# Eight transposes of a score tile in one go on TensorE, in a four-layer attention and expert kernel

## The chip, the cores and the metric

The kernel is one program on one core of a Trainium2 chip. The metric is the device time of one execution in microseconds (us), lower is better; the times shown are the median of several runs and their lowest and highest. The profile is one execution taken by the hardware profiler. In it PE is TensorE's matmuls, PEld its weight loads, DVE is VectorE, ACT is ScalarE, POOL is GpSimd, and SP is the engine that issues the DMAs.

## What is computed

The input `x` is 4 x 1024 x 128. Four layers follow, each `x = x + layer(layernorm(x))`: a first attention with relative positions (8 heads of 128), a mixture of 8 experts, a second attention (16 heads of 8, causal), and the same mixture of experts again. Only the first attention is touched:

```python
Q = (q @ w_qs).reshape(B, L, H, Dk).transpose(0, 2, 1, 3) * scale
K = (q @ w_ks).reshape(B, L, H, Dk).transpose(0, 2, 1, 3)
V = (q @ w_vs).reshape(B, L, H, Dv).transpose(0, 2, 1, 3)
attn = jnp.einsum('bnqd,bnkd->bnqk', Q + rel_embed_bias, K)
rel_k = (positions @ w_rel_pos_k).reshape(-1, H, Dk).transpose(1, 0, 2)
attn_pos = relative_shift(jnp.einsum('bnqd,nkd->bnqk', Q + rel_pos_bias, rel_k))
a = jax.nn.softmax(attn + attn_pos, axis=-1)
out = jnp.einsum('bnqk,bnkd->bnqd', a, V)
out = out.transpose(0, 2, 1, 3).reshape(B, L, H * Dv) @ w_out + b_out
```

With B = 4, L = 1024 and H = 8 that is 32 pairs of a head and a batch, each with a 1024 x 1024 score matrix.

## The kernel before, in words

**Tiles and steps.** A score tile is 128 queries by 1024 keys; there are 256 of them, `t` or `s` = 0 to 255, 32 for each head. The first attention runs as one long software pipeline with one step per tile (the loop over `s` in `plan_a`, L84). Four tiles make a quad (512 queries), `qd`; `kq = s % 4` is the place of a step in its quad. In step `s` the kernel computes the scores of tile `s`, the position products of tile `s + 3`, and a quarter of the product of the finished quad before it (`pq = s // 4 - 1`) with V.

**The order.** `plan_a` writes one list of units. PE, ACT, DVE and SP each walk through this same list and issue, for each unit, their own part of it, so that the list is the order of all of them; each waits on semaphores for what the others have to deliver. Nothing is reordered later: where an engine waits in one unit, its parts of all units behind it wait too. The units of a step, in order:

- `s`: six 512-wide matmuls give the scores in PSUM banks 2 and 3 (L612). DVE adds the position scores that a DMA brought into `a_sp`, and takes the minimum of the negated sum (L1201).
- `t` for `ja = 2 kq`: four 128 x 128 transposes (L622) turn one block of 128 keys of the quad's four tiles, into PSUM bank 4; ACT copies it to `a_Ph` in the rounded format (L904). Unit `tlow` is DVE's part: it takes the difference of the bank and `a_Ph` as the low half `a_Pl` (L1207). It stands behind `exp`.
- `pv` (block 7 of the quad before) where `kq` is 0, with ACT's copy of the finished sum to `a_osb` (L910).
- `r` 0: three 384-wide matmuls of the position products for tile `s + 3`; ACT copies them out (L889). `exp`: ACT's exponential of tile `s` (L897). `tlow` for `ja`. `r` 1: three more, copied out by DVE (L1193). `pv` for block `ja - 1`: three 512-wide matmuls with `a_Ph`, `a_Pl` and V (L635 to L637).
- one side unit in bank 7: the next quad's `q` (kq = 0), the transposes and the sum of the quad's output `out` (kq = 1, L643, L1222), a half of the next `k` (kq = 2) or of a `v` (kq = 3). `q`, `k` and `v` are matmuls, a rounded copy by ACT (`q`: two, L874; `k`: L879; `v`: L883) and the low half by DVE (`q`: two, L1174; `k`: L1180; `v`: L1186).
- `t` for `jb = 2 kq + 1`, into bank 5, with ACT's copy; `r` 2 and the DMA that writes the position products to DRAM; the DMA that reads them back skewed for tile `s + 2`; `tlow` for `jb`; `pv` for block `ja`.
- in some steps one or two `rel` units (the position blocks of the next head, also in bank 7), and in others the layer norms and gates of other layers.

**The waits at a transpose group.** Group `n = 8 pq + j` of PE waits until `p_lo` has reached `n - 1`, that is, until DVE has finished `tlow` of group `n - 2`, the last user of the same bank. ACT's copy of it waits until `pv` of block `n - 3` is through, since there are three buffers for `a_Ph`. The `r` 0 of the step with `kq` = 1 is the first that needs the quad's new `q`, and waits for both of its low halves.

```python
                if 8 * qd + j >= 2:
                    e.wait_ge(S["p_lo"], 8 * qd + j - 1)
                for k in range(4):
                    i = e.transpose(ps[:, 4 + j % 2, 128 * k:128 * k + 128],
                                    self.sp[:, (4 * qd + k) % NSP, 128 * j:128 * j + 128], ident[:, :])
```

Names in the rows: `a_sp` scores, `a_Ph` and `a_Pl` the two halves of the turned exponentials, `a_Qh`, `a_Kh`, `a_Vh` and `a_Ql`, `a_Kl`, `a_Vl` the halves of q, k, v, `a_rh` and `a_rl` of the position blocks, `a_rt` position products on their way to DRAM, `a_osb` the output sum, `a_fh` and `a_gh` what the position blocks are made of.

Of the kernel before, what the change touches and what calls it, by code (L numbers as in the profile page):

```python
# [51 lines left out]
def splits(p):  # L52

    return lambda b, bank: [("ln_stats", p, b), ("ln_total", p, b), ("ln_scale", p, b, 0), ("ln_turn", p, b, 0, bank),
                            ("ln_scale", p, b, 1), ("ln_turn", p, b, 1, bank)]


def gates(g, b):
    return [(u, g, b) for u in ("gt_logits", "gt_best", "gt_place", "gt_share", "gt_combine")]


def plan_a():

    p = splits(0)(0, 6) + [("x_bias", 0), ("feat",), ("wv", 0, 0, 7), ("q", 0, 2), ("k", 0, 0, 3), ("wv", 0, 1, 7),
                           ("k", 0, 1, 4)]
    p += [("rel", 0, u, 2 + (3 + i) % 5) for i, u in enumerate((7, 6, 5, 4))]
    p += [("v", 0, half, 2 + (2 + half) % 5) for half in range(2)]
    p += [("rel", 0, u, 2 + (4 + i) % 5) for i, u in enumerate((3, 2, 1, 0))]
    for t in range(3):
        p += [("r", t, 0), ("r", t, 1), ("r", t, 2), ("rout", t)]  # L70
        if t:
            p.append(("rin", t - 1))
    rel_at = {}
    for h in range(1, H):
        for ds, us in {-1: (7,), 1: (6,), 3: (5,), 4: (4, 3), 6: (2,), 8: (1,), 10: (0,)}.items():
            rel_at.setdefault(8 * (4 * h - 1) + ds, []).extend(("rel", h, u, 7) for u in us)
    extra = {}
    for b in range(1, B):
        for i, it in enumerate(splits(0)(b, 7) + [("x_bias", b)]):
            extra.setdefault(i // 4 if b == 1 else 8 * b - 14 + i, []).append(it)  # L80
    for b in range(B - 1):
        for i, it in enumerate(splits(1)(b, 7) + gates(0, b)):
            extra.setdefault(4 * (8 * (H - 1) + 2 * b + 3) + 1 + 3 * i // 4, []).append(it)
    for s in range(NTI + 6):  # L84
        kq, qd, bh, pq = s % 4, s // 4, s // 8, s // 4 - 1
        live, ahead, tlive = s < NTI, s + 3 < NTI, 0 <= pq < NQ
        ja, jb = 2 * kq, 2 * kq + 1
        h1 = s // 32 + 1
        if live and s % 32 == 2 and h1 < H:
            p.append(("load", h1))  # L90
        if live and s % 32 == 8 and h1 < H:
            p.append(("weights", h1))
        if live and s % 32 in (10, 12) and h1 < H:
            p.append(("wv", h1, s % 32 // 2 - 5, 7))
        if live:
            p.append(("s", s))
        if tlive:
            p.append(("t", pq, ja))
        if kq == 0 and 0 < pq <= NQ:
            p.append(("pv", pq - 1, 7))  # L100
        if ahead:
            p.append(("r", s + 3, 0))
        if live:
            p.append(("exp", s))
        if tlive:
            p.append(("tlow", pq, ja))
        if ahead:
            p.append(("r", s + 3, 1))
        if kq and tlive:
            p.append(("pv", pq, ja - 1))  # L110
        if kq == 0 and qd + 1 < NQ:
            p.append(("q", qd + 1, 7))
        if kq == 1 and 0 < pq <= NQ:
            p.append(("out", pq - 1, 7))
        if kq == 2 and live and bh + 1 < NTI // 8:
            p.append(("k", bh + 1, qd % 2, 7))
        if kq == 3 and live:
            if qd % 2 and bh + 1 < NTI // 8:
                p.append(("v", bh + 1, 0, 7))
            if qd % 2 == 0 and bh:  # L120
                p.append(("v", bh, 1, 7))
        if tlive:
            p.append(("t", pq, jb))
        if ahead:
            p += [("r", s + 3, 2), ("rout", s + 3)]
        if s + 2 < NTI:
            p.append(("rin", s + 2))
        if tlive:
            p += [("tlow", pq, jb), ("pv", pq, ja)]
        p += rel_at.get(s, []) + extra.get(s, [])  # L130
    return p
# [116 lines left out]
class Program:  # L248
    def __init__(self, nc, dram):
        self.nc, self.dr = nc, dram  # L250
        self.ctx = ExitStack()
        with self.ctx as ctx:
            self.S = {n: ctx.enter_context(nc.semaphore(n)) for n in SIGNALS}
            self.d_x = [ctx.enter_context(nc.semaphore(f"d_x{b}")) for b in range(B)]
            self.d_rout = [ctx.enter_context(nc.semaphore(f"d_rout{i}")) for i in range(4)]
            self.d_rin = [ctx.enter_context(nc.semaphore(f"d_rin{i}")) for i in range(NSP)]
            self.d_w1 = [ctx.enter_context(nc.semaphore(f"d_w1_{k}")) for k in range(E)]
            self.memory()
            self.plans = plan_a(), plan_f(0), plan_b(), plan_f(1)
            block = ctx.enter_context(nc.Block())  # L260
            block.sync(self.sync)
            block.tensor(self.tensor)
            block.scalar(self.scalar)
            block.vector(self.vector)
            block.gpsimd(self.gpsimd)
# [1233 lines left out]
```

## Time and profile before

| | us |
|---|---|
| device time, median of 3 runs | 3046.62 |
| lowest and highest | 3041.37, 3055.7 |
| the profiled execution's own device time | 3042.59 |
| its span in the trace | 3040.9 |
| PE busy | 2748.4 (90% of the span) |
| DVE busy | 2055.9 (68%) |
| ACT busy | 1735.5 (57%) |
| first attention | from the start to about 1700 |

Busy time of an engine is the union of its instructions, and a PE that is busy need not be at its peak. The timeline gives for each instruction its start, its length and its engine; matmuls overlap, so the pace of PE is read from one start to the next. "[1.42 <-DVE a_Ql L1174]" behind an instruction means that its engine stood idle for 1.42 us before it and which instruction ended that.

### The profile page before, as it was taken

What the parts mean: (1) busy time and instruction counts of PE and PEld (TensorE: products, weight loads), DVE (VectorE), ACT (ScalarE), POOL (GpSimd) and SP (SyncE); (2) the same over time, 40 slices, a digit from 0 to 9 for tenths busy, and PEclk for the clock granted to TensorE, in tenths of its full rate; (3) what the DMA queues carried; (4) which work ended last, traced back from release to release, by engine and by line L of the source; (5) the groups of instructions that cost most, each with busy time, mean ns of one, the idle gap of its engine ahead of it and who ended that gap; (6) DMA issues with size and microseconds to landing.
All of it is one profiled execution on the core that took longest, in us unless ns stands there. A gap on an engine that the chain in (4) does not pass through costs nothing. (4 is left out here: it accounts for less than half of the span.)

```text
span 3040.9 us, 46580 instructions
## 1 busy us (share of the span) xinstructions
PE 2748.4 (90%) x15120; PEld 2169.6 (71%) x15120; DVE 2055.9 (68%) x5219; ACT 1735.5 (57%) x3566; POOL 355.5 (12%) x782
## 2 busy tenths in 40 slices
PE   5999999999999999999999418998898999988999
PEld 4788888888888888888888316775555555554777
DVE  4766666666666666666666428887877777773887
ACT  3665666656666666666555214553666666655454
POOL 0000000000000000000000013341222122222344
PEclk8999999999999999999999759996999998999999
DMA  3554545545555455455443110000000000000000
GB/s 113 179 177 167 189 173 184 181 170 189 184 174 183 171 184 190 167 189 180 172 168 139 53 42 1 1 1 1 1 1 1 1 1 1 1 1 1 8 8 15
DMA packets 92673, 301.04 MB, mean 99 GB/s; under 512 B 10162, under 2 KB 24626, under 8 KB 92338
## 3 DMA queue, kind: packets, MB, share of 16 engines
q1 hardware_dynamic: 92434, 298.06, 28.5%
q8 instruction: 125, 2.05, 0.3%
q14 instruction: 114, 0.93, 0.1%
HBM read 144.93 MB, written 153.09 MB: 98 GB/s over the span
## 5 line engine op out<-in xcount | busy, mean ns | idle before, releaser
L904 ACT ACTIVATE a_Ph<-ps 128x512 fp32r<-128x512 f32 x512 | 305.9, 597 | 419.4 <-PE ps L622 415.0
L982 ACT ACTIVATE r_P<-ps 128x512 f32<-128x512 f32 (+3 forms) x768 | 328.0, 491 | 187.0 <-PE ps L752 182.7
L1201 DVE CUSTOM_DVE_ANT_0 a_sp<-ps,a_sp 128x1024 f32<-128x1024 f32 x256 | 313.1, 1223 | 176.9 <-PE ps L240 171.3
L1207 DVE TENSOR_TENSOR a_Pl<-ps,a_Ph 128x512 fp32r<-128x512 f32 x512 | 350.1, 684 | 11.4 <-ACT a_Ph L904 11.4
L933 ACT ACTIVATE r_y<-ps 128x256 f32<-128x256 f32 x512 | 194.3, 385 | 216.0 <-PE ps L666 213.7
L897 ACT ACTIVATE a_sp<-a_sp,a_nm 128x1024 f32<-128x1024 f32 x256 | 293.2, 1145 | 34.2 <-DVE a_nm L1201 34.1
L622 PE MATMUL ps<-ident,a_sp 128*128 128x128 f32 x2048 | 310.7, 274 | 0.0
L664 PE MATMUL ps<-r_Wh,p_xh 128*128 128x512 f32 x512 | 220.9, 431 | 93.9 <-DVE r_Wl L1236 46.6
L238 PE MATMUL ps<-a_rh,a_Qh 128*128 128x384 f32 x768 | 299.5, 390 | 4.7 <-DVE a_Ql L1174 4.2
L732 PE MATMUL ps<-r_K,r_Q 128*128 128x512 f32 (+3 forms) x768 | 282.7, 403 | 18.2 <-DVE r_mx L1363 12.8
L622 PEld LDWEIGHTS ps<-ident,a_sp 128*128 128x128 f32 x2048 | 250.2, 141 | 52.1 <-issue 1.0
L752 PE MATMUL ps<-r_Q,r_K 128*128 128x512 f32 (+3 forms) x768 | 254.2, 376 | 30.3 <-ACT r_P L982 28.4
L1363 DVE CUSTOM_DVE_ANT_0 ps<-ps,maskq 128x256 f32<-128x256 f32 (+3 forms) x512 | 244.8, 506 | 52.9 <-PE ps L732 51.8
L240 PE MATMUL ps<-a_rh,a_Ql 128*128 128x384 f32 x768 | 262.0, 341 | 0.0
L889 ACT ACTIVATE a_rt<-ps 128x384 f32<-128x384 f32 x512 | 252.9, 494 | 14.3 <-PE ps L240 13.7
L239 PE MATMUL ps<-a_rl,a_Qh 128*128 128x384 f32 x768 | 259.4, 338 | 0.0
L732 PEld LDWEIGHTS ps<-r_K,r_Q 128*128 128x128 f32 x768 | 145.1, 198 | 157.2 <-DVE r_mx L1363 80.0
L452 POOL TENSOR_TENSOR r_acc<-r_acc,r_yk 128x256 f32<-128x256 f32 x256 | 189.0, 738 | 329.2 <-DVE r_yk L1268 318.1
L464 POOL TENSOR_SCALAR_AFFINE_SELECT r_P<-r_P 128x128 f32<-128x128 f32 x512 | 153.1, 309 | 555.6 <-ACT r_P L982 547.3
L635 PE MATMUL ps<-a_Ph,a_Vh 128*128 128x512 f32 x512 | 210.0, 410 | 7.5 <-DVE a_Pl L1207 7.0
L440 POOL TENSOR_TENSOR wst<-wst,wr 128x512 f32<-128x512 f32 x4 | 5.0, 1262 | 1792.0 <-DMA wr<-in_w1r 1792.0
L1367 DVE TENSOR_REDUCE r_mx<-ps 128x1 f32<-128x512 f32 x256 | 176.1, 688 | 49.9 <-PE ps L732 48.5
(219 smaller groups left out, 6215.7 us busy)
## 6 DMA issues: line engine op xcount, KB each, us to landing
scr<-a_rt SPq DMA_DIRECT2D x256, 576.0 KB, 3.1
a_sp<-scr SPq DMA_DIRECT2D x256, 512.0 KB, 4.3
x<-in_q SPq DMA_DIRECT2D x4, 512.0 KB, 9.0
wst<-in_w1t SPq DMA_DIRECT2D x8, 256.0 KB
out<-x SPq DMA_DIRECT2D x4, 512.0 KB, 3.2
wr<-in_w1r SPq DMA_DIRECT2D x8, 254.0 KB
a_gst<-in_w_rel SPq DMA_DIRECT2D x8, 96.0 KB, 3.0
a_sp<-in_feat SPq DMA_DIRECT2D x1, 768.0 KB, 7.6
```

The lines of the kernel that those rows point to most:

```text
L238: e.matmul(out, lh, rh, start=True, stop=False)
L239: e.matmul(out, lh, rl, start=False, stop=False)
L240: return e.matmul(out, ll, rh, start=False, stop=True)
L622: i = e.transpose(ps[:, 4 + j % 2, 128 * k:128 * k + 128], self.sp[:, (4 * qd + k) % NSP, 128 * j:128 * j + 128], ident[:, :])
L732: e.matmul(ps[:, bank, 0:w], self.Q[:, b % 2, g, 128 * I:128 * I + 128], self.K[:, b % 2, q, 512 * part:512 * part + w], start=True, stop= ...
L752: e.matmul(ps[:, bank, off:512], self.K[:, b % 2, q, 128 * J:128 * J + 128], self.Q[:, b % 2, g, 512 * ch + off:512 * ch + 512], start=Tru ...
L889: e.activation(self.rt[:, t % 2, 384 * k:384 * k + 384], ps[:, (3 * t + k) % 2, 0:384], ACT.Copy).then_inc(S["r_act"], 1)
L897: e.activation(w, w, ACT.Exp, bias=self.nm[:, t % 8:t % 8 + 1], scale=-1.0, accum_out=self.ls[:, t % 16:t % 16 + 1]).then_inc(S["p_exp"], 1)
L904: e.activation(self.Ph[:, n % 3, :], ps[:, 4 + n % 2, :], ACT.Copy).then_inc(S["p_hi"], 1)
L982: e.activation(self.P[:, pt, off:512], ps[:, bank, off:512], ACT.Exp).then_inc(S["b_exp"], 1)
L1201: e.tensor_tensor_reduce(out=w, in0=ps[:, 2:4, :].rearrange("p a n -> p (a n)"), in1=w, scale=-1.0, scalar=3e38, op0=ALU.add, op1=ALU.min, ...
L1207: e.tensor_tensor(self.Pl[:, n % 3, :], ps[:, 4 + n % 2, :], self.Ph[:, n % 3, :].bitcast(F32), ALU.subtract).then_inc(S["p_lo"], 1)
```

## The change

The unit `t` for `jb` moves from behind the side unit to directly behind the `t` for `ja`. All other units keep their places, `tlow` and `pv` for `jb` among them.

```diff
         if tlive:
-            p.append(("t", pq, ja))
+            p += [("t", pq, ja), ("t", pq, jb)]
         if kq == 0 and 0 < pq <= NQ:
             p.append(("pv", pq - 1, 7))
...
                 p.append(("v", bh, 1, 7))
-        if tlive:
-            p.append(("t", pq, jb))
         if ahead:
             p += [("r", s + 3, 2), ("rout", s + 3)]
```

The lines of the changed kernel behind L121 have numbers smaller by 2. The following pieces are from the fourth head.

PE, a step with `kq` = 1, which has the `out` unit (L643), before:

```order
L622 MATMUL ps<-ident,a_sp 128x128 x4
L238 MATMUL ps<-a_rh,a_Qh 128x384
L239 MATMUL ps<-a_rl,a_Qh 128x384
L240 MATMUL ps<-a_rh,a_Ql 128x384
L238 MATMUL ps<-a_rh,a_Qh 128x384
L239 MATMUL ps<-a_rl,a_Qh 128x384
L240 MATMUL ps<-a_rh,a_Ql 128x384
L635 MATMUL ps<-a_Ph,a_Vh 128x512
L636 MATMUL ps<-a_Pl,a_Vh 128x512
L637 MATMUL ps<-a_Ph,a_Vl 128x512
L643 MATMUL ps<-ident,a_osb 128x128 x4
L622 MATMUL ps<-ident,a_sp 128x128 x4
```

and with the change:

```order
L620 MATMUL ps<-ident,a_sp 128x128 x8
L236 MATMUL ps<-a_rh,a_Qh 128x384
L237 MATMUL ps<-a_rl,a_Qh 128x384
L238 MATMUL ps<-a_rh,a_Ql 128x384
L236 MATMUL ps<-a_rh,a_Qh 128x384
L237 MATMUL ps<-a_rl,a_Qh 128x384
L238 MATMUL ps<-a_rh,a_Ql 128x384
L633 MATMUL ps<-a_Ph,a_Vh 128x512
L634 MATMUL ps<-a_Pl,a_Vh 128x512
L635 MATMUL ps<-a_Ph,a_Vl 128x512
L641 MATMUL ps<-ident,a_osb 128x128 x4
L236 MATMUL ps<-a_rh,a_Qh 128x384
```

The second group of transposes now stands ahead of nine matmuls and the output's transposes, instead of behind them.

ACT, a step with `kq` = 0, which has the copy of the output sum (L910) and the two copies of `q` (L874), before:

```order
L904 ACTIVATE a_Ph<-ps 128x512
L910 ACTIVATE a_osb<-ps 128x512
L889 ACTIVATE a_rt<-ps 128x384
L897 ACTIVATE a_sp,a_ls<-a_sp,a_nm 128x1024
L874 ACTIVATE a_Qh<-ps,a_bias 128x512 x2
L904 ACTIVATE a_Ph<-ps 128x512
L889 ACTIVATE a_rt<-ps 128x384
```

and with the change:

```order
L902 ACTIVATE a_Ph<-ps 128x512 x2
L908 ACTIVATE a_osb<-ps 128x512
L887 ACTIVATE a_rt<-ps 128x384
L895 ACTIVATE a_sp,a_ls<-a_sp,a_nm 128x1024
L872 ACTIVATE a_Qh<-ps,a_bias 128x512 x2
L887 ACTIVATE a_rt<-ps 128x384
```

The second copy to `a_Ph` now stands ahead of the exponential and of the two copies of `q`.

DVE keeps its order. From the same step with `kq` = 0 to the start of the next:

```order
L1193 COPY a_rt<-ps 128x384
L1174 SCALAR_TENSOR_TENSOR a_Ql<-ps,a_bias,a_Qh 128x512 x2
L1207 TENSOR_TENSOR a_Pl<-ps,a_Ph 128x512
L1201 ISA a_sp,a_nm<-ps,a_sp 128x1024
L1201 ISA a_nm 128x1
```

Nothing moved here: the second `a_Pl` of the step stands behind the two low halves of `q`.

## Rows read from the trace of the kernel before

**Rows 1.** Windows: busy us of PE, PEld, DVE, ACT, POOL, then clock, DMA

```profile
450.00:750.00 300.00, 294.77 (x1695) 260.02 (x1694) 195.27 (x375) 190.46 (x367) 0.00 (x0) 1.00 0.51 178
...
1350.00:1650.00 300.00, 286.84 (x1614) 250.86 (x1613) 196.06 (x438) 182.89 (x347) 0.00 (x0) 0.98 0.49 170
```

**Rows 2.** Waits of PE, 150 to 1700 us: total, times, longest

```profile
PE ps L238 <- DVE a_Ql L1174: 20.6, 15, 1.4
```

**Rows 3.** Timeline, PE, two steps: start, length, engine, line

```profile
995.14 0.40 PE L637 MATMUL ps<-a_Ph,a_Vl 128*128 128x512 f32 x1
...
1000.18 0.60 PE L622 MATMUL ps<-ident,a_sp 128*128 128x128 f32 x4
...
1000.54 0.42 PE L238 MATMUL ps<-a_rh,a_Qh 128*128 128x384 f32 x1
...
1000.80 0.34 PE L239 MATMUL ps<-a_rl,a_Qh 128*128 128x384 f32 x1
...
1000.97 0.34 PE L240 MATMUL ps<-a_rh,a_Ql 128*128 128x384 f32 x1
```

**Rows 4.** Timeline, ACT, the first of these steps

```profile
994.87 0.60 ACT L904 ACTIVATE a_Ph<-ps 128x512 fp32r<-128x512 f32 x1 [2.01 <-PE ps L622]
...
995.57 0.60 ACT L910 ACTIVATE a_osb<-ps 128x512 f32<-128x512 f32 x1
...
996.11 0.49 ACT L889 ACTIVATE a_rt<-ps 128x384 f32<-128x384 f32 x1
...
996.49 1.14 ACT L897 ACTIVATE a_sp<-a_sp,a_nm 128x1024 f32<-128x1024 f32 x1
...
997.62 1.26 ACT L874 ACTIVATE a_Qh<-ps,a_bias 128x512 fp32r<-128x512 f32 x2
```

**Rows 5.** Timeline, DVE, end of the first step

```profile
998.91 1.41 DVE L1174 SCALAR_TENSOR_TENSOR a_Ql<-ps,a_bias,a_Qh 128x512 fp32r<-128x512 f32 x2 [1.73 <-ACT a_Qh L874]
...
1000.24 0.68 DVE L1207 TENSOR_TENSOR a_Pl<-ps,a_Ph 128x512 fp32r<-128x512 f32 x1
```

**Rows 6.** Timeline, the same place in an early and a late quad

```profile
193.20 0.68 DVE L1207 TENSOR_TENSOR a_Pl<-ps,a_Ph 128x512 fp32r<-128x512 f32 x1
...
193.50 0.42 PE L238 MATMUL ps<-a_rh,a_Qh 128*128 128x384 f32 x1
...
1531.49 0.68 DVE L1207 TENSOR_TENSOR a_Pl<-ps,a_Ph 128x512 fp32r<-128x512 f32 x1
...
1531.79 0.42 PE L238 MATMUL ps<-a_rh,a_Qh 128*128 128x384 f32 x1
```

**Rows 7.** Timeline, bank 7: a position block behind q, one behind k

```profile
645.61 1.41 DVE L1174 SCALAR_TENSOR_TENSOR a_Ql<-ps,a_bias,a_Qh 128x512 fp32r<-128x512 f32 x2 [1.73 <-ACT a_Qh L874]
...
647.08 0.39 PE L238 MATMUL ps<-a_fh,a_gh 96*128 96x256 f32 x1 [1.42 <-DVE a_Ql L1174]
...
861.60 0.69 DVE L1180 TENSOR_TENSOR a_Kl<-ps,a_Kh 128x512 fp32r<-128x512 f32 x1 [1.23 <-ACT a_Kh L879]
...
862.43 0.31 PE L238 MATMUL ps<-a_fh,a_gh 96*128 96x256 f32 x1
```

**Rows 8.** Timeline, DVE and PE, a step with k

```profile
1010.20 0.68 DVE L1207 TENSOR_TENSOR a_Pl<-ps,a_Ph 128x512 fp32r<-128x512 f32 x1
...
1012.16 0.42 PE L238 MATMUL ps<-a_rh,a_Qh 128*128 128x384 f32 x1
```

**Rows 9.** Timeline and windows, output transposes with a score group behind them

```profile
1002.39 0.60 PE L643 MATMUL ps<-ident,a_osb 128*128 128x128 f32 x4
...
1002.82 0.60 PE L622 MATMUL ps<-ident,a_sp 128*128 128x128 f32 x4
...
1003.18 0.42 PE L238 MATMUL ps<-a_rh,a_Qh 128*128 128x384 f32 x1
...
1003.44 0.33 PE L239 MATMUL ps<-a_rl,a_Qh 128*128 128x384 f32 x1
...
1002.39:1003.18 0.79, 0.79 (x10) 0.79 (x8) 0.79 (x3) 0.79 (x2) 0.00 (x0) 1.00 0.82 239
```

## The prediction

> **What bounds the kernel now.** I read first the windows of the first attention, then PE's waits there, then the timeline of two neighbouring steps on PE, ACT and DVE. The windows [rows 1] show PE busy 294.77 of 300 us in the middle of the stage, and 286.84 of 300 near its end, at a granted clock of 1.00 and 0.98, with DVE at about 195 of 300 and ACT at 183 to 190. So PE's stream of matmuls sets the pace and hardly ever pauses. At 5.23 idle us in 300, a stage of some 1,600 us has about 28 us that any new order could bring back. Most of it is in [rows 2]: from 150 to 1700 us PE waits 20.6 us behind the low halves of q, in 15 places. No wait at a transpose group is among the waits. The gain of a change of order is bounded by these 28 us; its cost is whatever pauses it makes. The question is whether the second transpose group, moved forward by half a step, still finds its PSUM bank free and what its copy pushes back on ACT.
>
> **The work itself.** Nothing is added or removed: 2,048 transposes, 512 copies, 512 low halves, and the same matmuls and DMAs. A group of four is 0.36 us from its start to that of the next matmul (1000.18 to 1000.54 [rows 3]).
>
> **Step one, the bank.** Group jb writes bank 5, which is free when DVE has made the low half of the group two before, the jb of the previous step. That low half is the last thing DVE does in a step. Before, PE reached the group half a step later, so that it was always free. Now PE reaches it at the end of the ja group. In a step with kq = 1 the place is 1000.54, where the position products start before [rows 3]. The low half that it needs starts at 1000.24 and takes 0.68 [rows 5], so it ends at 1000.92, and would be 0.38 us late even if nothing else moved. The reason is the q unit of the step before: two copies on ACT, then two low halves on DVE from 998.91 for 1.41 us [rows 5], and only then the low half of jb. In [rows 6] the same distance is 193.88 less 193.50 = 0.38 in an early quad and 1532.17 less 1531.79 = 0.38 in a late one. It repeats from quad to quad. From a wait's end on DVE to PE's start I take 0.06: in [rows 7] the low halves of q end at 645.61 + 1.41 = 647.02, and the waiting block starts at 647.08.
>
> **Step two, ACT.** With kq = 0 the copy of jb now stands ahead of the output copy, the exponential and both copies of q. ACT works without a break through this part [rows 4]: the copy of ja starts at 994.87, the output copy at 995.57 (as soon as PE's last `pv` matmul, 995.14 + 0.40 [rows 3], is through), then 996.11, 996.49, and the copies of q at 997.62, where the exponential ends (996.49 + 1.14). The output copy becomes 0.36 later, since PE does the second group ahead of that `pv`. The second `a_Ph` copy fits in that time or just not: copies of this length follow each other at 0.54 (995.57 to 996.11), so they would allow the output copy at 994.87 + 2 x 0.54 = 995.95, and PE at 995.54 + 0.36 = 995.90. All behind it moves by about 0.36: the exponential, the copies of q, DVE's low halves of q, and the low half of jb. The bounds are 0 (if ACT made it up somewhere) and 0.60, one full copy; I take 0.36, because the chain has no idle time in which to make it up.
>
> So the pause is 0.38 + 0.36 + 0.06 = 0.80 us per quad. Behind the waiting transposes on PE stand the position products, `pv`, the output transposes and the next scores, so it is on the path in full. Which quads? There are 8 in each of 8 heads, 64. In two of the eight, position blocks stand behind q (two in one quad, one in the other); PE already waits for q there [rows 7], and DVE makes the low half of jb under the scores that follow. That leaves 48. In the last head two more quads carry layer norm and gate work that makes PE late anyway. In the timeline of the 46 that remain the low half ends 0.38 to 0.45 after the place. 46 x 0.80 = **36.8 us**.
>
> **Step three, bank 7.** Every side unit now runs 0.36 later in its step on PE, since the group stands ahead of it; the step's last `pv` ends where it did. A position block behind it waits for the low half of the side unit. Behind q PE waits already (1.42 us [rows 7]), and now 0.36 longer: in 14 places, 5.0 us. Behind k the low half ends at 861.60 + 0.69 = 862.29 and the block starts at 862.43 [rows 7]; with the 0.06 that leaves 0.08, so 0.36 becomes a pause of 0.28. I take the same for the blocks behind v and behind the output: 14 + 14 + 7 = 35 such blocks, 9.8 us (bounds 0 and 35 x 0.36 = 12.6). Together **14.8 us**.
>
> **Step four, what joining gives back.** The first matmul behind a group starts its follower after 0.26 (1000.54 to 1000.80), an ordinary one after 0.17 (1000.80 to 1000.97) [rows 3]. That looks like 0.09 for a turn-round, but the output's transposes with a score group right behind show what joining is worth: 1002.39 to 1003.44 is 1.05 [rows 9], and two separate groups, 2 x 0.62 less one ordinary matmul of 0.17, would be 1.07. Where kq = 1 such a pair existed and is now split, so nothing changes there. 192 other steps x 0.01 to 0.02 give back about **2 us** (bounds 0 and 192 x 0.09 = 17).
>
> **Elsewhere.** In the steps with k and v the low half of jb comes early enough: 1010.20 + 0.68 = 1010.88 against a place at 1012.16 [rows 8], 1.28 spare, of which 0.36 goes. The DMA queue of SP has the same order; a pause of PE gives its transfers more time. The rest of the program, from 1700 us on, is not touched. Sum: 36.8 + 14.8 - 2 = 49.6, on the profiled execution's 3042.6 that is 3092; on the median of the runs, 4 us higher, 3096. I take **3094 us**, 1.6% slower. A measurement of this kernel can tell about 0.5% (15 us) from no change.
>
> **A rule on the clock.** During the 0.79 us in which eight transposes already run in a row, the granted clock is 1.00, the level of 2.4 GHz [rows 9]; the windows of the whole stage, with all its groups of four, show the same [rows 1]. The Trainium skill (TensorE: Matmul & The Clock Gate, Part 4: PE-mode transpose) says that transposes do not count as a busy PE in the same way and that the full clock does not engage for them, which speaks against putting more of them in a row. By that rule the joined groups would run at the lower level; by the trace they do not.
>
> **The rivals.**
> Only the bank (0.08): ACT's shift vanishes, and so do the delays in bank 7. Then 46 x 0.44 = 20 us, 3063. Against it: ACT has no gap between 995.57 and the copies of q.
> More than one pause (0.05): the late quad start also makes the next odd group wait, a second 0.8 in each quad, 3042.6 + 49.6 + 37 = 3129. Against it stands the 1.28 of spare in the other steps.
> The clock (0.01): transposes at the lower level would take 0.11 us more each, at their present pace of 0.43 for four (1002.39 to 1002.82 [rows 9]); x 2,048 that is 225 us, 3268. The level in [rows 9] speaks against it.
> Not slower (0.04): joining saves the whole turn-round, 17 us, and PE's transposes do not stop at the bank because DVE gets its low half earlier, now that its `a_Ph` is ready long before. Then 3042.6 - 17 = 3026. The turn-round alone decides the sign only where the pause is under 17 / 46 = 0.37 us, and the bank alone makes it 0.44. Against the rest: on DVE q's low halves stay ahead of it, whatever ACT does.
> The change does nothing (0.02): something else fixes the place of the transposes. The order shows the eight in a row, so only an unseen reordering could do it; 3043.
>
> **How the numbers follow.** My forecast gets 0.80, its own range is 3080 to 3108 (bounds of ACT's shift, of step three, and the 4 us between profile and median). To hold 8 in 10 with these tails the range reaches down over the first rival: 3060 to 3110. Faster 0.02 (half of the not-slower case), same 0.05 (its other half, no effect, a small part of the first rival), slower 0.93.
>
> **What would show it.** In the changed profile the waits of PE should have a new line, transposes (L620) behind DVE's `a_Pl` (L1205) or behind q's low half, some 46 times at about 0.8, together 35 to 40 us; PE's waits behind `a_Ql` should grow from 20.6 to about 25, and new waits of about 0.3 appear for position blocks behind k, v and the output; ACT's copies of q should start about 0.36 later after the transposes than before; the clock stays at 1.00. I am wrong if PE shows no wait at the transposes, if the pause is near 0.4, or if it comes in every step.

## The result and the profile after

The changed kernel takes 3117.89 us, the median of four runs (3110.55 to 3127.2), against 3045.02 us for the kernel before (four runs, 3041.37 to 3055.7). The ratio is 1.0235, with a 95% interval of 1.0197 to 1.0273. It is slower, as forecast, but by 72.9 us where 49.6 were worked out, and it lies 8 us above the range of 3060 to 3110. The profiled execution took 3110.55 us, 68.0 more than that of before; it is the fastest of the four. All that is said below from a trace is said of one execution.

From the page of the changed kernel, its span, the engines' busy time and the group of the transposes (busy, mean ns of one, idle time before them and what ended it):

```profile
span 3108.8 us, 46580 instructions
...
PE 2776.5 (89%) x15120; PEld 2179.2 (70%) x15120; DVE 2071.0 (67%) x5219; ACT 1733.2 (56%) x3566; POOL 354.9 (11%) x782
...
L620 PE MATMUL ps<-ident,a_sp 128*128 128x128 f32 x2048 | 286.7, 281 | 35.5 <-DVE a_Pl L1205 35.5
```

The same 2,048 transposes are there. New is the last part: PE stood idle before them for 35.5 us, and DVE's low halves ended that. The windows answer to [rows 1], where PE was busy for 294.77 and 286.84 of 300 us:

```profile
450.00:750.00 300.00, 284.59 (x1595) 248.11 (x1594) 187.84 (x354) 177.51 (x344) 0.00 (x0) 0.99 0.49 170
...
1400.00:1700.00 300.00, 282.60 (x1579) 246.15 (x1578) 191.46 (x418) 175.34 (x335) 0.00 (x0) 0.98 0.48 164
```

PE's waits from 150 to 1780 us, as total, times and longest, answer to [rows 2]:

```profile
PE ps L620 <- DVE a_Pl L1205: 30.2, 45, 1.1
...
PE ps L236 <- DVE a_Ql L1172: 26.1, 14, 1.9
...
PE ps L236 <- DVE a_rl L1166: 6.5, 7, 0.9
...
PE ps L236 <- DVE a_Kl L1178: 2.7, 14, 0.2
...
PE ps L236 <- DVE a_Vl L1184: 1.6, 7, 0.2
```

The first line is the forecast one, 45 times: 42 waits of 0.63 to 0.66 us, and three of 1.1 in the last head. Three more, of 1.1 to 2.1, lie ahead of 150 us. Forecast were some 46 waits of about 0.8 and 35 to 40 us in all. The wait behind the low halves of q has grown from 20.6 to 26.1. The waits behind k and v are 0.2 us at the longest and small in sum, because an idle time in this view begins only where the modelled end of the matmul before lies. What a pause costs has to be read from starts.

The timeline of the two steps answers to [rows 3 to 5]. It is the same quad, now 41 us later:

```profile
1035.46 1.04 PE L620 MATMUL ps<-ident,a_sp 128*128 128x128 f32 x8
...
1036.25 0.48 PE L633 MATMUL ps<-a_Ph,a_Vh 128*128 128x512 f32 x1
...
1037.23 0.60 ACT L908 ACTIVATE a_osb<-ps 128x512 f32<-128x512 f32 x1
...
1039.27 1.25 ACT L872 ACTIVATE a_Qh<-ps,a_bias 128x512 fp32r<-128x512 f32 x2
...
1040.56 1.41 DVE L1172 SCALAR_TENSOR_TENSOR a_Ql<-ps,a_bias,a_Qh 128x512 fp32r<-128x512 f32 x2 [1.71 <-ACT a_Qh L872]
...
1041.39 0.60 PE L620 MATMUL ps<-ident,a_sp 128*128 128x128 f32 x4
...
1041.89 0.68 DVE L1205 TENSOR_TENSOR a_Pl<-ps,a_Ph 128x512 fp32r<-128x512 f32 x1
...
1042.62 0.66 PE L620 MATMUL ps<-ident,a_sp 128*128 128x128 f32 x4 [0.63 <-DVE a_Pl L1205]
...
1043.04 0.42 PE L236 MATMUL ps<-a_rh,a_Qh 128*128 128x384 f32 x1
```

Eight transposes start at 1035.46, and the next matmul at 1036.25. ACT's output copy comes 1.77 us behind the first transpose, where it came 995.57 - 994.23 = 1.34 behind it before, so that it is 0.43 later. In the second step four transposes start at 1041.39. The other four wait for the low half that starts at 1041.89, ends at 1042.57 and lets them go at 1042.62. This is the forecast pause at the forecast place.

To see the sum I compared, step by step, the start of the last score matmul of all 256 tiles in both traces. From the first to the last of them the changed kernel takes 77.7 us more. Of this, 47.0 us are in the steps with kq = 1, 11.1 with kq = 0, 13.0 with kq = 3, and 6.5 with kq = 2. Outside this stretch the profiled execution is some 10 us shorter than that of before, 3 us before the first tile, which the change does not touch, and 7 us after the last. Of these 7, 2.7 lie ahead of the last product with V, in steps that still hold joined groups, and 4 in the layers behind.

One thing in these steps was not in the forecast. In the second to the seventh head (the middle heads) the steps with s % 32 = 28 and 29 are 2.0 us longer together, where 0.36 was forecast. Before, the windows of step 28's quiet stretch and of what follows it are these (the last three columns are granted clock, DMA share and GB/s):

```profile
846.00:850.70 4.70, 2.34 (x14) 1.66 (x13) 2.43 (x4) 2.20 (x5) 0.00 (x0) 1.00 0.44 144
...
850.70:854.40 3.70, 3.70 (x22) 3.22 (x22) 2.76 (x7) 1.96 (x4) 0.00 (x0) 1.00 0.29 118
```

and with the change, with three rows of PE's timeline:

```profile
880.00:884.75 4.75, 1.94 (x12) 1.30 (x11) 2.43 (x4) 1.75 (x4) 0.00 (x0) 1.00 0.51 179
...
884.75:888.90 4.15, 4.15 (x18) 3.58 (x18) 2.21 (x6) 0.98 (x2) 0.00 (x0) 0.59 0.16 63
...
882.48 0.39 PE L236 MATMUL ps<-a_fh,a_gh 96*128 96x256 f32 x1 [1.88 <-DVE a_Ql L1172]
...
886.10 0.63 PE L237 MATMUL ps<-a_Kl,a_Qh 128*128 128x512 f32 x1
...
886.53 0.63 PE L238 MATMUL ps<-a_Kh,a_Ql 128*128 128x512 f32 x1
```

Before, the clock stayed at 1.00. Now it is 0.59 on average over 4.15 us: the granted clock goes to its level of 1.2 GHz for a while, and 512-wide matmuls start 0.43 us apart (886.10 to 886.53) instead of 0.23 (1034.08 to 1034.31 in the same trace). This happens once in each of the first seven heads; before it happened in one head of the seven.

### The profile page after: what moved, and what is told of

It is laid out like the page before. It is cut to its first block and busy times, and to the rows that moved or that the text cites. A ratio compares the mean times of both kernels' runs of the same rounds, so it can differ in the third digit from the quotient of the medians.

```text
span 3108.8 us, 46580 instructions
## 1 busy us (share of the span) xinstructions
PE 2776.5 (89%) x15120; PEld 2179.2 (70%) x15120; DVE 2071.0 (67%) x5219; ACT 1733.2 (56%) x3566; POOL 354.9 (11%) x782
## 5 line engine op out<-in xcount | busy, mean ns | idle before, releaser
L902 ACT ACTIVATE a_Ph<-ps 128x512 fp32r<-128x512 f32 x512 | 284.7, 596 | 460.7 <-PE ps L620 460.5
L620 PE MATMUL ps<-ident,a_sp 128*128 128x128 f32 x2048 | 286.7, 281 | 35.5 <-DVE a_Pl L1205 35.5
L236 PE MATMUL ps<-a_rh,a_Qh 128*128 128x384 f32 x768 | 286.9, 374 | 2.3 <-ACT a_rt L887 1.3
```

The costliest lines, as they stand in the source:

```text
L236: e.matmul(out, lh, rh, start=True, stop=False)
L620: i = e.transpose(ps[:, 4 + j % 2, 128 * k:128 * k + 128], self.sp[:, (4 * qd + k) % NSP, 128 * j:128 * j + 128], ident[:, :])
```

## The experiments

All are compared with runs of the kernel before made at the same time on the same chip. "Over before" is the difference of the medians. Not all experiments ran on one chip, so that two of them are compared by what each is over its own before. Each trace is again of one execution.

### Where the pause comes from

e1 joins the groups with kq = 1 only, e2 in all steps but those. The first edit is

```diff
         if tlive:
             p.append(("t", pq, ja))
+        if tlive and kq == 1:
+            p.append(("t", pq, jb))
...
-        if tlive:
+        if tlive and not (kq == 1):
             p.append(("t", pq, jb))
```

and e2 has `kq != 1` in both places.

> The two groups are joined only in the steps with kq = 1 (64 steps); all others keep the order of the kernel before. My theory: the group waits for DVE's low half, and half of the wait comes from the step with kq = 0, where ACT's chain is pushed back. Without that push the pause should be 0.38 late + 0.06 release + 0.06 restart = 0.50 us instead of about 0.86, in some 46 places: 23 us, and about 3 us more for the position block behind the output. Total about 26 us over the kernel before. Rival: the pause belongs to the kq = 1 step alone; then it stays at 0.86, about 43 us.

> The groups are joined in the steps with kq = 0, 2 and 3, and apart where kq = 1. My theory: no pause at any transpose group; the position products with kq = 1 wait about 0.15 us for the low halves of q, in some 46 places (7 us); the pauses of position blocks behind q, k and v stay as in the changed kernel (about 19 us), and so does the lower clock at the end of seven heads (about 11 us). Total about 35 to 40 us over the kernel before. Rival, that joining itself costs nothing outside kq = 1: under 10 us.

e1 took 3081.83 us, 35.6 over before (ratio 1.0118, 1.0102 to 1.0135); e2 took 3089.13, 42.9 over before (1.0138, 1.0121 to 1.0156). Two rows of e1, DVE's low half and the waiting group:

```profile
1022.21 0.68 DVE L1209 TENSOR_TENSOR a_Pl<-ps,a_Ph 128x512 fp32r<-128x512 f32 x1
...
1022.94 0.66 PE L624 MATMUL ps<-ident,a_sp 128*128 128x128 f32 x4 [0.19 <-DVE a_Pl L1209]
```

The low half ends at 1022.89, the group starts at 1022.94, and its step is 0.43 us longer than before; 0.50 was expected. In the changed kernel the same steps are 0.86 longer. So half of the pause belongs to the kq = 1 step alone, and the other half comes from the kq = 0 step. The rival of 0.86 falls. e1 is 35.6 over before where about 26 was expected, and the rest is not waits at the transposes: steps 28 and 29 together are 1.6 to 3.2 us longer in five heads, with the clock at the lower level, though the order of step 28 was not changed and its waits for q are as long as before. e2 is a little over the 35 to 40 expected. Its transposes wait in two places only (2.1 us), but the first position matmul behind the group with kq = 1 waits:

```profile
1034.08 1.41 DVE L1176 SCALAR_TENSOR_TENSOR a_Ql<-ps,a_bias,a_Qh 128x512 fp32r<-128x512 f32 x2 [1.71 <-ACT a_Qh L876]
...
1034.91 0.60 PE L624 MATMUL ps<-ident,a_sp 128*128 128x128 f32 x4
...
1035.64 0.41 PE L240 MATMUL ps<-a_rh,a_Qh 128*128 128x384 f32 x1
```

The low halves of q end at 1034.08 + 1.41 = 1035.49. That is the last thing the position products need, and they start at 1035.64, 0.73 behind the transposes' start instead of 0.36. The step is 0.34 longer, and 0.15 was expected. Two parts of the miss can be read. Both low halves of q end at 998.91 + 1.41 = 1000.32 [rows 5], and not at 1000.24, where the next instruction already starts beside them; and the matmul starts 0.15 behind their end (1035.49 to 1035.64), and not 0.06.

e3 leaves PE as in the changed kernel and moves DVE's low half of the second group ahead of those of q:

```diff
+        if kq == 0 and tlive:
+            p.append(("tlow", pq, jb))
         if kq == 0 and qd + 1 < NQ:
             p.append(("q", qd + 1, 7))
...
-            p += [("tlow", pq, jb), ("pv", pq, ja)]
+            p += ([("tlow", pq, jb)] if kq else []) + [("pv", pq, ja)]
```

> The changed kernel, but with kq = 0 DVE makes the low half of the second group ahead of the two low halves of q, in the 1.7 us in which it stood idle for them. My theory: the pause at the transposes is gone (46 x 0.86 = 40 us less than the changed kernel) and the low halves of q end as before, so that about 3077 to 3082 us remain. Rival (transposes are slow because of something else than this low half, or the low halves of q become late in turn and PE waits for them instead): within 10 us of the changed kernel's 3118.

It took 3084.26 us, 38.1 over before (1.0124, 1.0107 to 1.0141), where the changed kernel is 72.9 over. The low half is made in DVE's idle time, and the second step's transposes run through:

```profile
1023.29 0.68 DVE L1207 TENSOR_TENSOR a_Pl<-ps,a_Ph 128x512 fp32r<-128x512 f32 x1
...
1025.08 1.41 DVE L1174 SCALAR_TENSOR_TENSOR a_Ql<-ps,a_bias,a_Qh 128x512 fp32r<-128x512 f32 x2 [1.11 <-ACT a_Qh L874]
...
1025.91 0.93 PE L622 MATMUL ps<-ident,a_sp 128*128 128x128 f32 x7
```

The low half starts at 1023.29 and not behind q's at 1025.08. Seven of the eight transposes have a record, in one go from 1025.91 on, with no idle time. The steps with s % 32 = 13, 17 and 21 are as long as before the change. All steps with kq = 1 but those with s % 32 = 29 are together 3.7 us longer than before, where they are 40.9 us longer in the changed kernel. So the pause is the wait for this one low half, and it costs some 37 us (40.9 - 3.7). The time fell by 34.8, since e3's dips of the clock are twice as long as the changed kernel's (steps 28 and 29 are 3.5 us longer together, in six heads).

e4 leaves ACT's copy of the second group where it stood before:

```diff
+        if tlive:
+            p.append(("tcopy", pq, jb))
         if ahead:
             p += [("r", s + 3, 2), ("rout", s + 3)]
...
-            elif u[0] == "t":
+            elif u[0] == "t" and u[2] % 2 == 0 or u[0] == "tcopy":
```

> The changed kernel on PE, but ACT's copy of the second group stands where it stood before, behind the copies of q. My theory says that the 0.36 us of delay on ACT come from PE, which delivers the output sum one group later, and not from the copy itself, since the copy fits into that time: the time stays within 5 us of the changed kernel. Rival, the copy ahead of the exponential is what pushes q back: the pause falls from 0.86 to about 0.5 and the time by 15 to 20 us.

It took 3120.86 us, 74.7 over before, where the changed kernel is 72.9 over:

```profile
1044.17 1.25 ACT L874 ACTIVATE a_Qh<-ps,a_bias 128x512 fp32r<-128x512 f32 x2
...
1045.46 1.41 DVE L1174 SCALAR_TENSOR_TENSOR a_Ql<-ps,a_bias,a_Qh 128x512 fp32r<-128x512 f32 x2 [1.71 <-ACT a_Qh L874]
...
1047.52 0.66 PE L622 MATMUL ps<-ident,a_sp 128*128 128x128 f32 x4 [0.63 <-DVE a_Pl L1207]
```

The pause is there as before (0.63 idle, 0.84 in the length of the step). The copies of q start 5.19 us behind the step's first score matmul (1044.17 - 1038.98), exactly as in the changed kernel (1039.27 - 1034.08), although ACT has one copy less ahead of them; before, it was 4.76 (997.62 - 992.86). What pushes ACT is that PE delivers the output sum later. The place of the copy is without effect.

### Where the clock comes in

e5 joins the groups in the step with s % 32 = 28 alone; the edit is that of e1 with `s % 32 == 28`. This is the step in which two position blocks stand behind q.

> The groups are joined in one step of a head alone, the last with kq = 0 (s % 32 = 28), where two position blocks wait behind q. In the trace of the changed kernel this step and the next are 2.0 us longer together than before, of which 0.41 is the longer wait for q, and the granted clock falls to its lower level behind it in all seven heads that have such blocks. Theory (the longer idle time is followed by the lower clock): 7 x 2.0 = 14 us over the kernel before, with seven stretches of the lower level in the first attention. Rival (the dips come from the pauses in the other steps): 7 x 0.41 = 3 us and no more dips than before.

It took 3062.65 us, 17.4 over before (1.0062, 1.0042 to 1.0081), all of it around seven steps out of 256. The windows of the quiet stretch and what follows:

```profile
857.50:862.29 4.79, 2.00 (x11) 1.72 (x10) 2.43 (x4) 1.20 (x3) 0.00 (x0) 0.84 0.63 218
...
862.29:869.30 7.01, 7.01 (x29) 6.14 (x30) 3.53 (x9) 2.60 (x5) 0.00 (x0) 0.62 0.03 10
```

The clock is 0.62 on average over 7 us, in every one of the seven heads. Steps 28 and 29 are 3.4 us longer together, and only 0.41 of this is the longer wait. e6 takes the changed kernel and puts matmuls whose result nothing reads into the first gap of that step:

```diff
+        if s % 32 == 28 and s in rel_at:
+            p.append(("fill", 6))
...
+            elif u[0] == "fill":
+                for k in range(u[1]):
+                    e.matmul(ps[:, 4, :], self.wh[:, 0, 0, :], xh[:, 0:512], start=True, stop=True)
```

> The changed kernel with six more 512-wide matmuls per head in the idle time of 1.88 us behind q in that step, into bank 4, where nothing reads them. They take 6 x 0.23 = 1.4 us of it. Theory (idle time lowers the clock): the dips behind these steps vanish, and although there is more work the time falls by up to 7 x 1.6 = 11 us, to about 3107. Rival (the clock falls for another reason, or the matmuls delay what is behind them): the same or slower, 3118 or more, with the dips still there.

It took 3114.13 us, 68.9 over before, with the dips still there in six heads, so that my theory of one long wait failed. The step has a second gap of 0.93 us between the two blocks, with nothing but small matmuls around it. e7 came from the other side and was meant as the better kernel: q's matmuls and ACT's copies of q go ahead of the exponential, and DVE's low halves of q stay.

```diff
+        if kq == 0 and qd + 1 < NQ:
+            p.append(("q", qd + 1, 7))
         if live:
             p.append(("exp", s))
...
         if kq == 0 and qd + 1 < NQ:
-            p.append(("q", qd + 1, 7))
+            p.append(("qlow", qd + 1, 7))
...
-            elif u[0] == "q":
+            elif u[0] == "qlow" or u[0] == "q" and u[1] == 0:
```

> The kernel before, with q's matmuls and ACT's copies of q ahead of the exponential in the steps with kq = 0, DVE's low halves of q where they were. It should have the low halves of q ready about 0.9 us earlier, so that the 14 waits of 1.4 us shrink to 0.5: about 12 us less than before, and fewer dips of the clock at the end of a head (up to 1.6 us each). Rival: the exponential, 1.25 us later on ACT, makes the second a_Ph copy of the step late in turn, PE waits at pv in the next step, and the time stays within 5 us of the kernel before or rises.

It took 3021.92 us, 23.3 less than before (0.9932, 0.9907 to 0.9957). PE's waits behind the low halves of q:

```profile
PE ps L240 <- DVE a_Ql L1176: 8.6, 14, 0.6
```

They fell from 20.6 to 8.6 us, the 12 that were expected. The other half of the gain is not explained: of the 22.9 us by which the trace is shorter, the middle heads have 3.4, the first and the last together 12.5, and 8.3 lie behind the last tile (1.3 are lost before the first). Yet dips came behind steps 28 of six heads, with shorter waits than in the kernel before, where they came in one. The windows of such a stretch and of what follows:

```profile
837.43:842.13 4.70, 3.15 (x21) 2.43 (x19) 3.08 (x5) 3.39 (x7) 0.00 (x0) 1.00 0.19 77
...
842.19:846.00 3.81, 3.81 (x14) 3.12 (x14) 1.65 (x4) 0.49 (x2) 0.00 (x0) 0.55 0.59 194
```

PE was busy for 3.15 of the 4.70 us, more than the 2.34 of the kernel before, and the clock fell all the same. So neither the length of the wait nor the busy time of the stretch decides alone.

Then both gaps of that step were filled, six matmuls behind q and four between the blocks, in e5's kernel (e8), in the changed kernel (e9), and with four and four in e7's (e11):

```diff
-        p += rel_at.get(s, []) + extra.get(s, [])
+        rel = rel_at.get(s, [])
+        if s % 32 == 28 and rel:
+            rel = [("fill", 6), rel[0], ("fill", 4), rel[1]]
+        p += rel + extra.get(s, [])
```

> The kernel of e5 (joined in the one step with s % 32 = 28, seven long dips of the clock, 17 us over the kernel before), with both idle times of that step filled: six more 512-wide matmuls behind q and four between the two position blocks, 2.3 us of the 2.8 us idle, into bank 4. Theory (the quiet stretch as a whole, not its first gap alone, is what the dips follow): no dips at heads' ends, 7 x 3.1 = 22 us less of step time in the trace, about 3048. Rival (the dips have nothing to do with PE's idle time there): 3060 to 3063 with the seven dips.

> The changed kernel with the same two fills. Theory: the dips go, 7 x 1.6 = 11 us less than the changed kernel's 3118, about 3107; what stays over the kernel before is the 40 us of pauses at the transposes and about 25 us of waits in bank 7. Rival: as e6, dips in six or seven heads and 3114 to 3118.

e8 took 3044.19 us (0.9995 of before, 0.9982 to 1.0007). With 70 more matmuls than e5 it has lost all of e5's 17.4 us:

```profile
847.50:852.02 4.52, 4.05 (x22) 2.87 (x20) 2.43 (x4) 1.52 (x4) 0.00 (x0) 1.00 0.55 185
...
852.02:857.80 5.78, 5.78 (x36) 5.15 (x36) 4.55 (x13) 3.54 (x7) 0.00 (x0) 1.00 0.13 51
```

PE is busy for 4.05 us of a stretch in which it was busy for 2.00 of 4.79 in e5, and the clock stays at 1.00 behind it. All that is left is 0.41 us in step 28 of each head, the longer wait. In e9 the same happens behind step 28, but the time, 3114.26 us, is 68.2 over before, 4.7 less than the changed kernel where 11 was expected:

```profile
886.05:891.80 5.75, 5.75 (x35) 5.16 (x35) 4.16 (x12) 3.44 (x7) 0.00 (x0) 1.00 0.12 50
...
908.90:913.59 4.69, 2.83 (x15) 2.23 (x14) 2.48 (x4) 3.12 (x7) 0.00 (x0) 1.00 0.21 88
...
913.59:917.80 4.21, 4.21 (x19) 3.55 (x18) 1.74 (x4) 0.98 (x3) 0.00 (x0) 0.59 0.63 196
```

The first row, behind step 28, is at 1.00. The second is the next quiet stretch, in the step with s % 32 = 0, which has one block behind q and a wait of 1.86 us. In the third, behind it, the clock now falls in five heads, where it had stayed up. e12 fills this gap too, with six matmuls.

> The changed kernel with the two fills of e9 and a third of six 512-wide matmuls in the 1.88 us of idle time behind q in the step with s % 32 = 0, where the dips of e9 had moved to. Theory: no dips at or behind heads' ends, about 1.6 us less per head than the changed kernel, 11 us in all in the trace, about 3105 to 3108; what is left over the kernel before is about 62 us of waits. Rival (a dip comes once per head in any case and only moves on): 3114 again, with the dips in a third place.

It took 3107.39 us, 64.7 over its before (1.0208, 1.0187 to 1.0230), and the dips of the first seven heads are gone:

```profile
PE ps L625 <- DVE a_Pl L1213: 30.2, 45, 1.1
...
882.42:888.19 5.77, 5.77 (x35) 5.15 (x35) 4.18 (x12) 3.47 (x7) 0.00 (x0) 1.00 0.16 58
...
909.96:914.50 4.54, 4.54 (x30) 4.05 (x29) 2.99 (x7) 2.90 (x6) 0.00 (x0) 1.00 0.55 181
```

Both stretches are at 1.00, and the pauses at the transposes are what they were. The step-by-step difference from before is 66.9 us against 77.7 for the changed kernel. So the clock cost some 11 us, about 1.6 us in each of seven heads, and waits and all else the other 67. The two ways to count agree to about 2 us: the kernel before has a dip of 1.6 us in its first head, which e12 lacks. The medians say 8 us (72.9 less 64.7).

> The kernel before with seven more 512-wide matmuls once, in step 20, which shifts all that follows by 1.6 us and changes nothing else. In e7 the waits at the heads' ends were shorter than before and dips came nonetheless, so that I suspect that it matters when the quiet stretch falls. Theory: the number of dips at heads' ends differs from the one of the kernel before (up to seven, up to 3 us each): 3047 to 3065. Rival (only the length of the quiet stretch counts): 3047, with none or one.

e10 adds a fill of seven matmuls to the kernel before, once in step 20. It took 3050.86 us, 1.0019 of before (1.0006 to 1.0032), 4.8 us above for 1.6 us of work. The profiled execution had no dip in the first seven heads, but it is the fastest of the ten (3040.48 to 3056.16), so that its trace says little of the others. This neither bears out nor refutes that it matters when the quiet stretch falls.

> The kernel of e7 (3022) with four 512-wide matmuls behind q and four between the blocks in that step. If the quiet stretch is what the dips follow, its six dips go: about 8 us less than e7, 3014. Rival: no change or 2 us more, since the work in the gaps delays the blocks.

e11 took 3020.17 us, 0.9917 of before (0.9896 to 0.9938). The dips at heads' ends are gone in its trace, where steps 28 are 0.78 shorter than before and 29 unchanged, but it is 25.9 us below its before and e7 23.3 below its own, a difference of 2.6 us where about 8 was expected, and less than the runs spread. It is the fastest kernel here beside e7, and e7 is the simpler one.

## Why the prediction was right and wrong

**Direction and mechanism.** The forecast case happened: the second group reaches bank 5 before DVE has made the low half, once per quad, at kq = 1, in 42 quads, and ACT's chain adds to it. e1, e3 and e4 show it. The rivals "only the bank", "more than one pause", "not slower" and "no effect" did not happen. The clock rival did not either as it was put, since the clock is 1.00 over nearly a whole head of the changed kernel, full of groups of eight, between two dips:

```profile
470.00:670.00 200.00, 192.09 (x1088) 167.66 (x1086) 126.48 (x235) 122.52 (x236) 0.00 (x0) 1.00 0.51 174
```

By the rule of the Trainium skill weighed there (TensorE: Matmul & The Clock Gate, Part 4: PE-mode transpose) they would run at the lower level; no run here shows it.

**Step one and two: 36.8 us, measured 36 to 37, by luck.** The length of a group was wrong. I took 0.36 us, the distance to the start of the next matmul [rows 3], but that matmul then starts its own follower 0.08 later; a whole group costs 0.43, and that stood in [rows 9] (1002.39 to 1002.82). Eight transposes took 0.79. So ACT moved by 0.41 to 0.43 and not 0.36. A second thing was missing: PE starts slowly after a pause. Four transposes behind one take 0.42 to the next start (1042.62 to 1043.04), not 0.36. The pause is then 1000.92 + 0.41 + 0.06 - 1000.61 + 0.06 = 0.84, and the steps show 0.86 where 0.80 was forecast. But there are 42 such quads and not 46: in the first head three quads and in the last one more have no such pause, or a longer wait that costs less. 42 x 0.86 = 36.1, and the comparison with e3 gives 37. Too short a pause and too many places cancelled.

**Step three, bank 7: 14.8 us, measured 20, and 4.7 left out.** The same two errors of size came in here. A position block behind v in the changed kernel:

```profile
873.30 0.69 DVE L1184 TENSOR_TENSOR a_Vl<-ps,a_Vh 128x512 fp32r<-128x512 f32 x1 [2.06 <-ACT a_Vh L881]
...
874.05 0.38 PE L236 MATMUL ps<-a_fh,a_gh 96*128 96x256 f32 x1
...
874.51 0.40 PE L236 MATMUL ps<-a_Kh,a_Qh 128*128 128x512 f32 x1
```

The low half ends at 873.99, the block starts at 874.05, and it takes 0.46 to the next start, against 0.38 for the block in [rows 7], whose next start is 862.81. The steps with a block behind k or v are 0.44 longer (28 places, 12.3 us), those behind the output 0.27 (7 places, 1.9 us), those behind q 0.41 (14 places, 5.8 us). Left out altogether were the two units of the next head's `wv` weights, which also use bank 7, behind the output and behind a v: 0.24 and 0.44 in each of seven heads, 4.7 us.

**Step four, joining: 2 us back, measured none.** The steps without a wait are 0.02 us shorter in some places, and the steps with a v unit are 0.05 longer. Together they come to nothing that I can name.

**The clock: 0 us, measured 11.** This is the step of the prediction that failed: the clock was to stay at 1.00, and so it was put at nothing in the sum. It is the largest error. Without these 11 us the median would be at about 3107, inside the range (an estimate: 3117.89 less 11). I had read the level only where PE's work was dense, took the two waits behind q at the end of a head as 1.42 us each, to become 0.36 longer, and did not look at the clock behind them.

37 + 20 + 4.7 + 11 = 73 of the 77.7 us of step time. The 5 us that remain, most of them in the first and the last head, the 10 us by which the rest of the profiled execution was shorter, and the 5 us by which the median difference is above that of the two profiled executions have no cause shown here. That runs of one kernel differ by so much goes in part with the clock: of 23 runs of the kernel before on one chip, the fastest, 3036.51 us, had a mean granted clock of 0.956 and the slowest, 3054.41 us, 0.947. The range was too narrow for one more reason: its upper end was built from the bounds of named terms, with 0.05 for more than one pause and nothing for terms left out.

## What to carry to other kernels

Before a producer is moved forward in an in-order stream, look for who empties its buffer and what stands ahead of that on its own engine: here the low half of a block stood behind a longer job that had nothing to do with it. Measure a group of matmuls by the distance between starts of the same kind, add the restart after a pause, and list every user of a shared bank, the rare ones too. And before pauses are added to a stretch of PE that is already quiet, look at the granted clock behind it, since a stretch that just held the clock may no longer.

## What was unexpected of the hardware

The granted clock fell behind a stretch of small matmuls and waits, 2.00 us busy in 4.79 in e5, with no idle time above 1.9 us in it, and stayed up when 4.05 of 4.52 us were busy in e8. But about the same quiet stretch kept it in six of seven heads of the kernel before (2.34 busy of 4.70) and lost it in six of seven of e1, where it was unchanged (2.34 of 4.70), and of e7, where its waits were shorter and PE was busier (3.15 of 4.70). When the first such stretch of a head was filled (e9), the next one lost it, which it had not done before in these heads. What decides between them stays open; e10 was to tell it and did not. A dip lengthened its steps by 1.6 to 3.1 us, so that over seven heads a change elsewhere could move the time by an estimated 11 to 22 us through the dips alone.
